# Recommendation tower on one core: the waits ahead of the embedding gathers, made finer and moved

## The reference, cut to what matters

```python
e = stack([tbl_f[ids[:, f]] for f in range(32)], axis=1)      # 1024 samples, 32 fields, 64 floats each
idx_i, idx_j = triu_indices(32, k=1)                          # 496 pairs of fields
z = sum(einsum('bpd,pde->bpe', e[:, idx_i], W) * e[:, idx_j], axis=-1)   # W: 496 x 64 x 64
h = concatenate([z, dense_ctx], axis=1)                       # 1024 x 512
h = maximum(h @ W_top1 + b_top1, 0)                           # 512 -> 512
h = maximum(h @ W_top2 + b_top2, 0)                           # 512 -> 256
y = h @ W_top3                                                # 256 -> 1
```

## Time and profile before

| | |
|---|---|
| time, median of 3 runs | 583.75 us (582.8 to 584.56) |
| the profiled execution | 586.02 us, its span 584.1 us |
| granted TensorE clock, mean | 0.88 |
| ACT busy | 331.8 us (57%) |
| POOL busy | 294.5 us (50%) |
| indirect gathers (line 596) | 256, 944 ns each on POOL |
| all DMA | 18.86 MB, mean 32 GB/s |

### The profile page before, as it was taken

How to read it: one execution, slowest core, us unless ns; L and a number is a source line. 1 busy time by engine, 2 the same in 40 slices (tenths; PEclk the granted TensorE clock), 3 DMA queues, 4 the chain that set the end, 5 groups by cost and what they waited for, 6 DMA issues and landing times.

```text
span 584.1 us, 8849 instructions
## 1 busy us (share of the span) xinstructions
PE 421.7 (72%) x2440; PEld 223.8 (38%) x2440; DVE 333.8 (57%) x289; ACT 331.8 (57%) x2479; POOL 294.5 (50%) x356
## 2 busy tenths in 40 slices
PE   0140059468857697669988789177989799999998
PEld 0030023224433343335444344043545355445546
DVE  0000047446656475556578577056688689988780
ACT  0000047368478266762574569355558689789862
POOL 6777535555544463445545434655555406667240
PEclk9985569679779797888979989678999999999999
DMA  8999401211100010011101000101101000000000
GB/s 140 170 168 163 80 12 35 68 21 20 21 14 17 19 21 15 19 19 19 20 13 22 16 16 13 25 19 19 20 19 21 17 3 2 2 1 2 2 1 0
DMA packets 44679, 18.86 MB, mean 32 GB/s; under 512 B 39764, under 2 KB 40280, under 8 KB 44632
## 3 DMA queue, kind: packets, MB, share of 16 engines
q1 hardware_dynamic: 36120, 8.86, 11.6%
q0 software_dynamic: 8512, 9.45, 8.4%
HBM read 18.29 MB, written 0.00 MB: 31 GB/s over the span
## 4 chain that ended last, share of the span: by engine, by line
PE 34%; DVE 7%; another core or an unknown queue 6%; issue 3%; ACT 0%; DVEq 0%; ACTq 0%
PE left L816 10%; PE left L811 10%; PE z_sum L837 5%; DVE z_nat L672 2%; DVE row_products L663 2%; PE turned L855 2%; PE turned L776 1%; PE turned L877 1%; PE left L824 1%; PE left L855 1%; DVE column_products L643 1%; DVE column_products L651 1%; DVE column_products L655 1%; PE turned L886 1%
## 5 line engine op out<-in xcount | busy, mean ns | idle before, releaser
L596 POOL DMA_INDIRECT rows<-in_tbl_dram,ids_sb x256 | 241.6, 944 | 212.5 <-DVE column_products L655 77.4
L708 ACT ACTIVATE row_products<-row_products 128x64 f32<-128x64 f32 x1200 | 287.3, 244 | 22.7 <-issue 18.0
L708 ACT ACTIVATION_READ_ACCUMULATOR row_products<-row_products 128x1 f32 x1200 | 228.4, 190 | 18.8 <-issue 18.4
L655 DVE TENSOR_TENSOR column_products<-left,X 128x1024 f32<-128x1024 f32 x104 | 125.2, 1218 | 118.0 <-remote 86.5
L663 DVE TENSOR_TENSOR row_products<-left,rows 128x1024 f32<-128x1024 f32 x120 | 143.0, 1217 | 80.5 <-remote 38.9
L816 PE MATMUL left<-w_sb,X 64*128 64x512 f32 x480 | 138.1, 669 | 68.4 <-issue 54.2
L811 PE MATMUL left<-X,w_sb 64*128 64x256 f32 x960 | 141.9, 428 | 55.9 <-DVE row_products L663 30.7
L811 PEld LDWEIGHTS left<-X,w_sb 64*128 64x128 f32 x960 | 101.2, 211 | 116.4 <-DVE row_products L663 42.8
L691 ACT ACTIVATE X<-turned 128x512 f32<-128x512 f32 (+1 forms) x34 | 19.3, 567 | 144.4 <-remote 72.7
L816 PEld LDWEIGHTS left<-w_sb,X 64*128 64x128 f32 x480 | 44.7, 201 | 114.9 <-issue 84.3
L613 POOL TENSOR_TENSOR row_products<-row_products 128x512 f32<-128x512 f32 (+4 forms) x75 | 45.4, 606 | 52.8 <-DVE row_products L663 48.1
(11 more groups left out here) (30 smaller groups left out, 80.5 us busy)
## 6 DMA issues: line engine op xcount, KB each, us to landing
rows<-in_tbl_dram,ids_sb POOLq DMA_INDIRECT x256
w_sb<-in_W_top_dram SPq DMA_DIRECT2D x1, 512.0 KB
w_sb<-in_L_rec_W_dram SPq DMA_DIRECT2D x1, 496.0 KB
w_sb<-in_L_rec_W_dram SPq DMA_DIRECT2D x1, 480.0 KB
w_sb<-in_L_rec_W_dram SPq DMA_DIRECT2D x1, 464.0 KB
w_sb<-in_L_rec_W_dram SPq DMA_DIRECT2D x1, 448.0 KB
w_sb<-in_L_rec_W_dram SPq DMA_DIRECT2D x1, 432.0 KB
w_sb<-in_L_rec_W_dram SPq DMA_DIRECT2D x1, 416.0 KB
```

The costliest lines, as they stand in the source:

```text
L596: pool.indirect_dma_start(out=rows[:, q % 2 * QT + t, f * D:(f + 1) * D], out_offset=None, in_=tables[f], in_offset=bass.IndirectOffsetOnA ...
L655: nc.vector.tensor_tensor(to, of, X[:, n:n + 2, :].rearrange("p g b -> p (g b)").unsqueeze(1).to_broadcast([P, 2, BANK]), ALU.mult).then_i ...
L708: ins = nc.scalar.activation(product, product, ACT.Copy, accum_out=z_nat[:, tile, column:column + 1])
```

## The change

Each single gather now may have a wait of its own (GROUP = 1), for a count that depends on its number g of 0 to 255: the larger of (g - 32) x 0.95 and, in the first quarter (g < 64), (g - 16) x 0.5, rounded down. Up to g = 79 it is capped by WITHIN, the number of pieces of a quarter that need only field pairs gathered at least three groups earlier (LAG), so that no gather waits for a piece that needs it. Worked out, the counts are:

- g 0 to 23: 0; 24 to 27: 1; 28 to 31: 3; 32 to 35: 5; 36 to 39: 7; 40 to 43: 10; 44 and 45: 14; 46 and 47: 15
- then about one more per gather: 16 at g = 48, 29 at g = 63, 60 at g = 96, 91 at g = 128, 152 at g = 192, 211 at g = 255

The waits ahead of the third and fourth quarter stay. The planner's model of the gathers is rewritten to follow single gathers (3.5 us to the first, 1.25 us each, 6.0 us to land, in place of 5.0 us for four and 9.5 us to land), and X_WAIT and MLP_WAIT go down by four. So the written order of the other engines, and which engine makes which row sum, may change too. No arithmetic, tile or transfer is added or removed.

```diff
-X_WAIT, MLP_WAIT = 14, 20
+X_WAIT, MLP_WAIT = 10, 16
-GATHER, LANDING, W_FIRST, W_PAIR = 5.0, 9.5, 6.0, 0.1
+GATHER_FIRST, GATHER, LANDING, W_FIRST, W_PAIR = 3.5, 1.25, 6.0, 6.0, 0.1
...
-PACED, PIECES_APART = 12, 3.4
-def pieces_before(q, m):
-    n = FP * q + FP - 1 - m
-    return max(0, int((n - PACED) * PIECES_APART))
+GATHERS = 4 * FP * QUARTERS
+GROUP, AHEAD, APART, LAG = 1, 32, 0.95, 3
+FIRST_AHEAD, FIRST_APART = 16, 0.5
+def first_gather(q, m):
+    return 4 * (FP * q + FP - 1 - m)
+def within(m):
+    columns, rows = make_work()
+    return sum(min(k for k, _ in x[2]) >= m if x[0] == "columns" else x[2] >= m for x in columns[:COLUMN_PIECES]) \
+        + sum(x[3] >= m for x in rows[:ROW_PIECES])
+WITHIN = [within(FP - n) for n in range(FP + 1)]
+def pieces_before(g):
+    if g % GROUP:
+        return 0
+    n = int(max((g - AHEAD) * APART, (g - FIRST_AHEAD) * FIRST_APART if g < 4 * FP else 0))
+    if g // 4 - LAG <= FP:
+        n = min(n, WITHIN[max(0, g // 4 - LAG)])
+    return max(0, n)
...
     def landed(self, q, m):
-        end = GATHER * (FP * q + FP - m)
...
-        return end + LANDING
+        last = first_gather(q, m) + 3
+        while len(self.gathered) <= last:
+            g = len(self.gathered)
+            begin = self.gathered[-1] if g else GATHER_FIRST
+            if g == first_gather(1, FP - 1):
+                begin += CHUNKS * GATHER
...
+            n = pieces_before(g)
+            if n > len(self.end):
+                return None
+            if n:
+                begin = max(begin, self.end[n - 1] + SIGNAL)
+            self.gathered.append(begin + GATHER)
+        return self.gathered[last] + LANDING
...
                 for m in range(FP - 1, -1, -1):
-                    if pieces_before(q, m):
-                        pool.wait_ge(multiplied, pieces_before(q, m))
-                    for t in range(QT):
-                        for f in (2 * m, 2 * m + 1):
-                            pool.indirect_dma_start(
...
+                    for n in range(4):
+                        t, f = n // 2, 2 * m + n % 2
+                        before = pieces_before(first_gather(q, m) + n)
+                        if before:
+                            pool.wait_ge(multiplied, before)
+                        pool.indirect_dma_start(
...
```

More of the change, by code:

```diff
@@ L170, in __init__ @@
         self.fill, self.held, self.x_work = None, False, 0
-        self.end = []
+        self.end, self.gathered = [], []
         self.left = [0.0] * RING
@@ L186, in landed @@
     def landed(self, q, m):
-        end = GATHER * (FP * q + FP - m)
-        if q >= 2:
-            if not self.done(q - 2):
-                return None
[L192 to L197, removed]
-        return end + LANDING
+        last = first_gather(q, m) + 3
[4 more added lines that the diff above has]
+                begin += CHUNKS * GATHER
+            if g in (first_gather(2, FP - 1), first_gather(3, FP - 1)):
+                before = g // (4 * FP) - 2
+                if not self.done(before):
+                    return None
+                begin = max(begin, max(e for e, x in zip(self.end, self.work) if x[1] == before) + SIGNAL)
+            n = pieces_before(g)
+            if n > len(self.end):
+                return None
+            if n:
+                begin = max(begin, self.end[n - 1] + SIGNAL)
+            self.gathered.append(begin + GATHER)
+        return self.gathered[last] + LANDING
     def on_pe(self, what, begin, length):
@@ L590, in _ @@
                 for m in range(FP - 1, -1, -1):
-                    if pieces_before(q, m):
-                        pool.wait_ge(multiplied, pieces_before(q, m))
-                    for t in range(QT):
-                        for f in (2 * m, 2 * m + 1):
-                            pool.indirect_dma_start(
-                                out=rows[:, q % 2 * QT + t, f * D:(f + 1) * D], out_offset=None, in_=tables[f],
-                                in_offset=bass.IndirectOffsetOnAxis(ap=ids_sb[:, QT * q + t, f:f + 1], axis=0),
-                            ).then_inc(rows_gathered[q % 2][m], 16)
+                    for n in range(4):
[4 more added lines that the diff above has]
+                        pool.indirect_dma_start(
+                            out=rows[:, q % 2 * QT + t, f * D:(f + 1) * D], out_offset=None, in_=tables[f],
+                            in_offset=bass.IndirectOffsetOnAxis(ap=ids_sb[:, QT * q + t, f:f + 1], axis=0),
+                        ).then_inc(rows_gathered[q % 2][m], 16)
             halvings = 0
```

## The result

The changed kernel takes 523.87 us (median of 4 runs, 518.8 to 524.1) against 584.15 (4 runs): ratio 0.895, interval 0.889 to 0.901. Forecast were 463 us and a range of 430 to 550. So it is faster, by 60 us where 121 were forecast.

The account below looks back on a forecast made before the run. The bound was taken to be PE once gathers leave the engines alone; until 460 us long unbroken series hold PE, ACT and DVE. Sum: 140 + 255 + 63 + 5 = 463 us, range 430 to 550.

Parts of the forecast that it names:

- no harm at all: Rival, chance 0.08: paced gathers do not slow the engines; 217/0.95 = 228 us, start 10 us better, 426 us.
- (b): First quarter: piece 1 at 41 us, gather 44 at 70, last row asked for at 91, quarter ends about 140.
- (c): After the first quarter: 217 us of PE work beside gathers at 0.85 take 255 us, the rest 63 us.
- The feedback that I named: Gathers on POOL: if the pieces stop, so do the gathers, and the hold ends.
- The tail: After gather 255, which waits for piece 211: 37 pieces and a set of layers at 0.95 full, 63 us.
- (f): POOL's row sums after the last gather: about eight of 15 go to DVE or ACT, 0 to 10 us, taken as 5.
- The sign set for (f): End of the kernel: the last 60 pieces slower than 1.33 us each would show wrong the row-sum cost forecast.
- The rival of density: Chance 0.20: density of gathers counts, not series length; the stretch runs at 0.59, 547 us, with a slow start 550.
- (d): POOL: 208 more waits; one already met costs nothing, one just met 0.27 us in place of 0.30 of issue; hidden.
- (g): X_WAIT and MLP_WAIT four lower: at most some 40 more switches of 0.20 us, 8 us; taken as 0.
- (e): Rows in time, tightest mid-quarter: 14 pieces or 20 us ahead where about 10 are needed; 32 ahead is enough.
- The rival that the holes had another cause than gathers: Chance 0.04: the holes do not come from gathers; pieces run as before, 584 us within a few us.

Follow-up runs that it names:

- after_again: The changed kernel, unchanged, run again in one set with the kernel before, with traces, without holds: 426.28 us, ratio 1.001.
- land4: The changed kernel, with GpSimd from the second quarter on also waiting, ahead of each field pair's four gathers, until the four before have landed: 515.02 us, ratio 0.881.
- probe2: Separate kernel, not the tower: free ScalarE, VectorE and TensorE streams beside gathers in phases, TensorE's stream shortened against the first probe: 1117 us.
- before_again: The kernel before, unchanged, run again with a trace, without holds: 426.01 us, ratio 1.000.
- group4: The changed kernel with waits only ahead of each fourth gather (GROUP = 4), same counts: 426.34 us, ratio to before 1.001.
- first_only: The changed kernel's waits in the first quarter, the kernel before's waits (groups of four, 48 ahead, 0.85 per gather) after it: 432.28 us, ratio 1.015.
- later_only: The changed kernel with the first quarter's waits as in the kernel before, single waits from the second quarter on: 425.43 us, ratio 0.999.
- ahead48: The changed kernel with single waits but the kernel before's counts from the second quarter on, (g - 48) x 0.85: 551.63 us, ratio 0.941.

## Why the prediction was half right

**What bounds the kernel.** Right, and now shown: the same program without holds takes 426 us, with PE busy 237 of 240 us in the middle. The prediction's case "no harm at all" came to 426, and its parts hold too: 130, 228 and 68 us for the first quarter, the stretch to piece 211 and the tail, where after_again has 128, 225 and 71.

**(b) The start** was right up to gather 44 (first piece 38.5 us, forecast 41; gather 44 at 72.4, forecast 70). Then it was too good: gather 63 at 100.6 us, not 91, and the 33 pieces after it took 66 us, not 47 (without holds 43). Piece 62 came at 167 us, not 140: 27 us.

**(c) The stretch beside the gathers** is the term that was mis-sized, here and in (b). 217 us of PE work at 0.85 were to take 255 us; they took 285, which is 0.76. I took the rate from 410 to 450, where fours with breaks ran, and assumed that single waits would keep single gathers apart. They don't: 178 of 260 transfers ran in series of five or more. A wait on finished pieces spaces the gathers only if the pieces are evenly spaced, and after each stop they come faster than that. The feedback that I named does exist (a held engine stops the gathers after a few), and that it bounds a series is why the third piece comes at 40.7 us, and why after the first quarter, which ends with eleven transfers in a row, no series is longer than eight. But it bounds it only after the harm has begun. The granted clock of the stretch 140 to 380 was 0.94, without holds 0.99, so a part of the missing rate is the clock.

**The tail** after piece 211 took 70.0 us; 63 and the 5 of (f) were forecast. In the kernel before it took 69.5 us, with holds and without: the 63 was 7 us too low and (f) cost nothing. The sign set for (f) (the last 60 pieces slower than 1.33 us each) was met, at 1.64, but it did not show (f): the last 37 pieces took 1.47 us each in both kernels. Start 27, stretch 30, tail 2: that is the miss of 59 us of span.

**The signs set.** Met was the third piece by 45 us, and nearly so no idle time over 5 us (DVE one of 5.2, ACT two of 5.9). Not met were the 62nd piece by 140, gathers one by one, no instructions of ACT spread out to 0.7 us, a PE strip of 8s and 9s and a clock near 1.0.

**Length or density.** The table above speaks for length: in land4, 179 of 260 transfers run in series of up to four, about as dense as in the changed kernel, and hold ACT for 2.0 us in all; the 81 in longer series hold it for 14.2. In the four kernels a transfer of a longer series costs ACT 3.7 to 16 times as much as one of a short series. What this does not settle is PE and DVE: with fours forced apart DVE works at 0.79 and not 0.89. Of the 240 us, 11.5 go to late rows, without which it would be at 0.83 (estimate, 189/228.5); the rest is open. The rival of density, 547 to 550 us, was nearer to the 524 measured than the forecast of 463 was, but by its slow start and not by its mechanism: it gave the stretch to piece 211 339 us, the forecast 255, measured 285.

**(d), (f), (g) Side costs.** Summed they were forecast at 5 us, bounds 0 to 18. A sum on POOL is six instructions, not five, and POOL has 30 fewer (326 against 356). Without holds the two kernels differ by 0.1%, interval -0.5 to +1.2 us: 208 more waits, five row sums fewer on POOL (10 against 15; four went to DVE and one to ACT, eight were forecast) and the new order cost nothing together. With holds only the tail above tells of them.

**(e) The data in time.** Right for the changed kernel: past the first pieces PE waits once for rows at a transpose, 3.0 us at 50.3 us with holds. land4 shows where the bound is: there rows were late.

**The rule weighed.** By the Trainium skill, "SBUF — State Buffer", "Who interferes with whom", gathers can't hold PE or ACT. Without holds every trace agrees with it (probe2: 238 ns in all phases; 192 gathers in a row beside a full PE). With holds the traces disagree: what happened to PE at 414 us is above. What is held is the start of instructions, not their run (ACT 249 against 240 ns each). The rival that the holes had another cause than gathers is half alive: the gathers are what brings them on, but something else decides whether they can.

**Open.** What makes the machine hold. It is not the chip by itself (before_again without, land4 with holds, the same chip), nor the program, nor the time a gather takes (0.94 us in both). The trace of the kernel before speaks against a lack of fetched instructions: fetches lie at 358.4, 362.0 and 390.1 us, the hold ends at 380, and ACT's instructions are 0.24 us apart again from there on, before any further fetch. What the chip's other cores did at the time is in no trace. No run could set it off or take it away. And group4, first_only and later_only, which were to part the gain of the first quarter from that of the single waits, all ran without holds, so that parting rests on land4 and ahead48.

## What to carry to other kernels

Measure the kernel before again beside every experiment: here it was 584 us in one set and 426 in the next, and a change worth 10% in one was worth nothing in the other. A wait that counts the consumer's work paces a producer only as evenly as the consumer works; where what must be bounded is a run of transfers, bound that run itself, and check that the data aren't late then. And look at the start first: with holds, 36 of the 62 us of gain stood by the third piece (40.7 us, before 77), after the gathers had been stopped for the first time.

## What the runs showed of the hardware

With holds, PE and ACT issue about one instruction each 0.70 us from 5 to 8 us into most unbroken series of six or more gathers until 1 to 3 us after them; the instructions themselves are as long as ever, and the DMA engines are busy 9 to 11% of the time (140 to 380 us). An engine that has stood still is not held so: 25 us into the first series of the changed kernel PE issues 28 matmuls, from 28.8 to 35.5 us, one each 0.21 us but for the wait for `X`. Without holds 192 gathers in a row, 1.25 us each, leave PE busy 179.9 of 180 us. The first rows land some 10 us after their gathers beside the weights; holding the weights back made the first piece 4 us earlier, and the kernel no faster.
